# A transformer layer on one core: the feed-forward columns computed only for the tokens that chose them, in sorted order

## What is computed

```python
q = q * cos + rotate_half(q) * sin                 # k likewise
att = softmax(causal((q @ k.T + bias) / sqrt(16)))  # per head
attention = (att @ v) @ Wp + bp

logits  = l2norm(xn) @ l2norm(col_emb).T + sigmoid(gelu(xn @ gate_w1 + gate_b1) @ gate_w2 + gate_b2)
mask    = one_hot(top_1(logits), 16)                # k = max(1, int(16 * 0.05)) = 1
weights = mask * softmax(logits)
cols    = gelu(einsum("bsd,cdn->bscn", xn, W_cols) + b_cols) * weights[..., None]
y       = cols.reshape(-1, 1024) @ proj_w + proj_b + xn
ffn     = layernorm(y) * ln_g + ln_b
```

## Time and profile before

| | |
|---|---|
| median of 3 runs | 2119.47 us (2115.34 to 2126.33) |
| profiled execution | 2120.78 us |
| its span in the profile | 2118.7 us |
| PE busy | 1881.9 us |
| DVE busy | 1602.9 us |
| ACT busy | 1101.7 us |
| POOL busy | 632.2 us |
| first score product | 220 us into the span |
| mean granted PE clock | 0.962 |

### The profile page before, as it was taken

How to read it: one execution, slowest core, us unless ns; L and a number is a source line. 1 busy time by engine, 2 the same in 40 slices (tenths; PEclk the granted TensorE clock), 3 DMA queues, 4 the chain that set the end, 5 groups by cost and what they waited for, 6 DMA issues and landing times.

```text
span 2118.7 us, 41887 instructions
## 1 busy us (share of the span) xinstructions
PE 1881.9 (89%) x11110; PEld 1051.4 (50%) x11110; DVE 1602.9 (76%) x5859; ACT 1101.7 (52%) x2142; POOL 632.2 (30%) x848
## 2 busy tenths in 40 slices
PE   4887899999999999999999999999999999997677
PEld 2654455555445555555455554455555554443223
DVE  2335788888888688878888778887888788887773
ACT  2231555555565555556555455565555555644444
POOL 5463333223333322233333123333332233300000
PEclk9988899999999999999999999999999999998887
DMA  8422212232222122232212222221222322112101
GB/s 221 130 60 76 59 50 65 56 84 81 66 60 72 49 68 64 60 93 68 59 47 69 70 75 66 65 76 47 70 56 64 86 81 60 47 52 58 45 14 41
DMA packets 199400, 144.77 MB, mean 68 GB/s; under 512 B 60427, under 2 KB 186779, under 8 KB 199148
## 3 DMA queue, kind: packets, MB, share of 16 engines
q1 hardware_dynamic: 199148, 141.85, 24.2%
HBM read 90.59 MB, written 56.69 MB: 70 GB/s over the span
## 4 chain that ended last, share of the span: by engine, by line
PE 58%; DVE 21%; issue 11%; POOL 3%; SPq 3%; ACT 3%; DMA 1%; DVEq 0%; ACTq 0%; POOLq 0%
PE scores L1081 10%; PE bank L1092 9%; PE o_bank L1000 8%; PE scores L983 7%; PE bank L1038 5%; DVE scores L1153 5%; PE rows L1020 4%; DVE rows L1178 4%; PE rows L1026 3%; DVE maxima L1174 3%; PE rows L1024 2%; PE scores L1083 2%; PE bank L1110 2%; DVE maxima L1183 2%; ACT probs L869 2%
## 5 line engine op out<-in xcount | busy, mean ns | idle before, releaser
L869 ACT ACTIVATE probs<-scores 128x512 f32<-128x512 f32 (+1 forms) x1280 | 670.7, 555 | 522.5 <-DVE scores L1153 238.4
L983 PE MATMUL scores<-stack_q,stack_k 99*128 99x512 bf16 (+3 forms) x1536 | 439.0, 337 | 85.2 <-ACT probs L869 60.4
L1178 DVE CUSTOM_DVE_ANT_0 rows<-rows,near_rows 128x256 f32<-128x256 f32 (+1 forms) x1024 | 416.1, 409 | 28.3 <-PE rows L1020 24.6
L1153 DVE TENSOR_TENSOR scores<-scores,near_cols 128x256 f32<-128x256 f32 x768 | 333.6, 443 | 84.5 <-PE scores L983 84.0
L1174 DVE TENSOR_REDUCE maxima<-rows 128x1 f32<-128x256 f32 (+1 forms) x768 | 304.9, 397 | 121.4 <-PE rows L1024 119.3
L1000 PE MATMUL o_bank<-probs,v_aug 128*32 128x512 f32 (+3 forms) x3072 | 320.7, 505 | 3.2 <-ACT probs L869 3.2
L1020 PE MATMUL rows<-stack_k,stack_q 96*128 96x256 bf16 (+1 forms) x1024 | 276.2, 276 | 41.5 <-DVE maxima L1178 24.0
L1081 PE MATMUL scores<-xn_t,w_cols 128*128 128x256 f32 x1024 | 286.9, 404 | 2.5 <-ACT others_t L915 2.5
L1183 DVE TENSOR_REDUCE maxima<-rows 128x1 f32<-128x128 f32 (+3 forms) x512 | 248.9, 486 | 50.3 <-PE rows L1026 48.1
L1092 PE MATMUL bank<-w_proj,act_t 128*128 128x256 f32 x1024 | 270.4, 402 | 16.4 <-DVE y L1211 14.7
L983 PEld LDWEIGHTS scores<-stack_q,stack_k 99*128 99x128 bf16 x1536 | 142.3, 99 | 217.4 <-ACT probs L869 138.1
(11 more groups left out here) (109 smaller groups left out, 2270.2 us busy)
## 6 DMA issues: line engine op xcount, KB each, us to landing
parts_d<-part SPq DMA_DIRECT2D x96, 256.0 KB, 2.5
stack_q<-parts_d SPq DMA_DIRECT2D x384, 64.0 KB, 2.6
stack_k<-parts_d SPq DMA_DIRECT2D x384, 64.0 KB, 2.6
x<-in_x_dram SPq DMA_DIRECT2D x32, 256.0 KB, 3.5
v_d<-v SPq DMA_DIRECT2D x32, 256.0 KB, 2.5
rest_d<-rest SPq DMA_DIRECT2D x32, 256.0 KB, 2.7
v_in<-v_d SPq DMA_DIRECT2D x32, 256.0 KB, 3.3
result<-rest_d SPq DMA_DIRECT2D x32, 256.0 KB, 3.9
```

The costliest lines, as they stand in the source:

```text
L869: act.activation(probs[:, (g * NS + s) % PROBS, h, 0:width], ring[(rings + ring_n[1]) % RING][:, 0:width], ACT.Exp, scale=float(D) ** -0.5 ...
L983: ins = pe.matmul(ring[(rings + ring_n[1]) % RING][:, c0:c0 + w], stack_k[g % 2][:, h, kb * P:(kb + 1) * P], stack_q[g % 2][:, h, q0:q0 + ...
L1153: dve.tensor_tensor(tile[:, 0:2 * P], tile[:, 0:2 * P], near, ALU.add))
L1178: dve.tensor_tensor_reduce(tile[:, 0:w], tile[:, 0:w], near_rows[:, ag * GH + h, 2 * P - w:2 * P], 1.0, LOWEST, ALU.add, ALU.max, maxima[: ...
```

## The change

The dense feed-forward part is replaced by a sorted one. When the fourth chunk of a batch has passed the gate (group 2), `tally` and `route` count the tokens of each column (PE products with matrices of ones, DVE arithmetic), give each column whole halves of 64 slots, and each token a slot; 2048 slots a batch, whatever the choice. POOL scatters the 1024 rows of xn to `xs_d` (8 indirect transfers). The following four groups each take 512 slots (`FFN_STEPS`): SP loads them (`ffn_in`), PE turns them (`xs_turn`), `neurons` and `columns` compute each half with its own column's weights, which POOL has gathered one group ahead from a table in DRAM (8 indirect transfers, `weights`), ScalarE scales by the weight, POOL adds xs, SP stores `ys_d`. POOL gathers the rows back by token (`gather`, 2 x 4 transfers); `finish_begun`, `finish_stats` and `finish` do the layer norm just ahead of `project`, and x is read again from DRAM (`again`) in place of `rest_d`. Further: row tiles are packed (`ROW_TILES`, 10 instead of 12 a head, 7 instead of 10 plain reductions), the last two value products, `o_out` and `o_turn` of a group move into the opening of the next (`TAIL`), `shift` moves to slot 34, `shift_turn` to 36, the load of v to its own stage at 28, the store of the parts to slot 37 (`parts`), and POOL's rotation writes into `rot` without the tile `swapped`.

```diff
+SLOT = 64
+WROW = KC * N + C + 1
+SLOTS_B = (T // SLOT + E) * SLOT
+FFN_STEPS = NC
+HALVES = SLOTS_B // SLOT // FFN_STEPS
+PAIRS = HALVES // 2
...
-ROWS = [(qb, part) for qb in range(NT) for part in range(1 if qb < 4 else 2)]
-EARLY = [k for k, (qb, _) in enumerate(ROWS) if qb < NT // 2]
-LATE = [k for k, (qb, _) in enumerate(ROWS) if qb >= NT // 2]
+ROW_TILES = [
+    ([(0, 0, 128, 0), (1, 0, 256, 256)], [("near", 0, 0), ("near", 1, 256)]),
+    ([(2, 128, 384, 0), (3, 256, 512, 256)], [("near", 2, 0), ("near", 3, 256)]),
+    ([(2, 0, 128, 0), (3, 0, 256, 256)], [("far", 2, 0, 128, 1, 1), ("far", 3, 256, 256, 1, 1)]),
+    ([(4, 384, 640, 0), (5, 512, 768, 256)], [("near", 4, 0), ("near", 5, 256)]),
+    ([(6, 640, 896, 0), (7, 768, 1024, 256)], [("near", 6, 0), ("near", 7, 256)]),
+    ([(4, 0, 384, 0)], [("far", 4, 0, 384, 1, 1)]), ([(5, 0, 512, 0)], [("far", 5, 0, 512, 1, 1)]),
+    ([(6, 0, 384, 0)], [("far", 6, 0, 384, 1, 1)]), ([(7, 0, 512, 0)], [("far", 7, 0, 512, 1, 1)]),
+    ([(6, 384, 640, 0), (7, 512, 768, 256)], [("far", 6, 0, 256, 2, 2)])]
+EARLY, LATE = range(3), range(3, len(ROW_TILES))
...
-BESIDE = {1: [('columns', 3)],
-          2: [('widen', None), ('columns', 4)],
-          3: [('center', None)],
-          4: [('columns', 5)],
-          5: [('columns', 6)],
-          6: [('columns', 7)],
-          7: [('x_turn', None)],
-          9: [('y2_stats', None)],
-          10: [('skip', None)],
+ROUTE_STEPS = 14
+WT_LOADS = HALVES
+BESIDE = {2: [('widen', None)],
+          3: [('finish_begun', 0)],
+          6: [('center', None), ('finish_stats', 0)],
+          8: [('x_turn', None)],
+          9: [('finish', 0)],
           11: [('qk_begun', 0), ('qk', 0)],
-          12: [('load_q', None), ('v', 0)],
-          15: [('finish', None), ('qk_begun', 1)],
-          16: [('qk', 1)],
-          17: [('hidden', None)],
-          19: [('v', 1)],
+          12: [('load_q', None)],
+          13: [('v', 0), ('finish_begun', 1)],
+          14: [('xs_turn', 0), ('qk_begun', 1)],
+          15: [('qk', 1)],
+          16: [('xs_turn', 1), ('finish_stats', 1)],
+          18: [('neurons', None), ('hidden', None)],
+          19: [('v', 1), ('finish', 1)],
           21: [('gate', None), ('o_turn', 0)],
+          22: [('columns', 0), ('gather', 1)],
           23: [('qk_turn', 0), ('choose', None)],
+          24: [('columns', 1)],
           25: [('left', 0), ('tie', None), ('middle', 0)],
-          26: [('choice', None), ('y_turn', 0)],
-          28: [('load_k', None), ('project_begun', 0)],
-          29: [('project', 0)],
-          30: [('qk_turn', 1)],
-          31: [('left', 1), ('mask_turn', None)],
-          32: [('y_turn', 1)],
-          34: [('middle', 1)],
-          35: [('project_begun', 1)],
-          37: [('project', 1)]}
-OPENING = [("stats", None), ("columns", 0), ("columns", 1), ("columns", 2)]
-ALONE = ([("stats", None), ("center", None), ("x_turn", None)] + [("columns", k) for k in range(C_PIECES)]
-         + [("qk_begun", 0), ("qk", 0), ("qk_begun", 1), ("qk", 1), ("y2_stats", None), ("skip", None),
-            ("hidden", None), ("v", 0), ("gate", None), ("v", 1), ("choose", None), ("qk_turn", 0),
-            ("left", 0), ("tie", None), ("choice", None), ("finish", None), ("middle", 0), ("qk_turn", 1),
-            ("left", 1), ("mask_turn", None)]
-         + [("neurons", (k, m)) for k in range(2) for m in range(N_PIECES)] + [("middle", 1)]
-         + [("neurons", (k, m)) for k in range(2, 4) for m in range(N_PIECES)])
-CLOSING = [("load", None), ("neurons", (0, 0)), ("neurons", (0, 1)), ("pv", NS - 1), ("o_out", 1),
-           ("neurons", (1, 0)), ("neurons", (1, 1)), ("neurons", (2, 0)), ("shift", None),
-           ("neurons", (2, 1)), ("neurons", (3, 0)), ("neurons", (3, 1)), ("o_turn", 1), ("shift_turn", None)]
+          26: [('choice', None), ('y_turn', 0), ('weights', 0)],
+          27: [('weigh', None), ('gather', 0), ('weights', 1), ('qk_turn', 1)],
+          28: [('load_k', None), ('load_v', None), ('project_begun', 0), ('tally', None), ('weights', 2)],
+          29: [('project', 0), ('left', 1), ('weights', 3)],
+          30: [('weights', 4)],
+          31: [('middle', 1), ('route', None)],
+          32: [('y_turn', 1), ('weights', 5)],
+          33: [('weights', 6), ('weights_routed', 0), ('weights_routed', 1)],
+          34: [('shift', None), ('project_begun', 1), ('weights', 7), ('weights_routed', 2), ('weights_routed', 3)],
+          35: [('weights_routed', 4), ('weights_routed', 5)],
+          36: [('project', 1), ('shift_turn', None), ('weights_routed', 6), ('weights_routed', 7)],
+          37: [('parts', None)]}
+OPENING = [("again", 0), ("ffn_in", None), ("stats", None)]
+ALONE = [("stats", None), ("center", None), ("x_turn", None), ("qk_begun", 0), ("qk", 0), ("qk_begun", 1), ("qk", 1),
+         ("hidden", None), ("v", 0), ("gate", None), ("v", 1), ("choose", None), ("qk_turn", 0), ("left", 0),
+         ("tie", None), ("choice", None), ("weigh", None), ("middle", 0), ("qk_turn", 1), ("left", 1), ("tally", None),
+         ("route", None)] + [("weights", i) for i in range(HALVES)] + [("middle", 1), ("parts", None)]
+FFN_ALONE = ([("ffn_in", None), ("xs_turn", 0), ("xs_turn", 1), ("neurons", None), ("columns", 0), ("columns", 1)]
...
+CLOSING = [("load", None)]
+TAIL = {-2: ("pv", NS - 2), -1: ("pv", NS - 1), 1: ("o_out", 1), 4: ("o_turn", 1)}
...
+                    elif stage == "route":
+                        pool.wait_ge(slots_ready, fb + 1)
+                        alone(pool)
+                        wait(pool, ffn_loaded, fb * (FFN_STEPS * 16))
+                        alone(pool)
+                        if g < 0:
+                            pool.wait_ge(columns_in, LATE_LOADS * 16)
+                        for j in range(NT):
+                            pool.indirect_dma_start(xs_d[:, :], bass.IndirectOffsetOnAxis(slot_i[:, j:j + 1], 0),
+                                                    xn_all[:, j, :], None).then_inc(scattered[j >= CT], 16)
...
+                    elif stage == "weights":
+                        yb, k, step = next_step(b, g)
+                        if arg == 0:
+                            pool.wait_ge(columns_routed, yb + 1)
+                            alone(pool)
+                        pool.indirect_dma_start(wt[:, arg, :], None, wt_d[:, :],
+                                                bass.IndirectOffsetOnAxis(
+                                                    weight_at[:, k * HALVES + arg:k * HALVES + arg + 1], 0)) \
+                            .then_inc(wt_in, 16)
...
+                    elif stage == "gather":
+                        if arg == 0:
+                            wait(pool, gathered, b * (NT * 16))
+                            alone(pool)
+                            pool.tensor_copy(slot_kept[:, :], slot_i[:, :]).then_inc(slots_kept, 1)
+                            pool.wait_ge(slots_kept, b + 1)
+                            alone(pool)
+                            pool.wait_ge(ys_out, (b + 1) * (FFN_STEPS * 16))
+                            alone(pool)
+                        wait(pool, finished, b * NC + 2 * arg)
+                        alone(pool)
+                        for j in range(NT // 2):
+                            at = arg * (NT // 2) + j
+                            pool.indirect_dma_start(gathered_y[:, j, :], None, ys_d[:, :],
+                                                    bass.IndirectOffsetOnAxis(slot_kept[:, at:at + 1], 0)) \
+                                .then_inc(gathered, 16)
...
+                    elif stage == "columns":
+                        yb, k, step = step_of(b, g)
+                        pool.wait_ge(scaled_ys, step * 2 + (arg + 1))
+                        pool.tensor_tensor(ys[:, 2 * arg:2 * arg + 2, :], ys[:, 2 * arg:2 * arg + 2, :],
+                                           xs[:, 2 * arg:2 * arg + 2, 0:C], ALU.add).then_inc(ys_ready, 1)
...
+                    elif stage == "ffn_in":
+                        yb, k, step = step_of(b, g)
+                        if k == 0:
+                            sp.wait_ge(scattered[0], (yb + 1) * (CT * 16))
                             alone(sp)
-                            sp.dma_start(result[:, k], rest_d[b, :, k * CT:(k + 1) * CT, :]) \
-                                .then_inc(rest_in_done[k], 16)
+                            sp.wait_ge(scattered[1], (yb + 1) * ((NT - CT) * 16))
+                            alone(sp)
+                        wait(sp, ys_out, step * 16)
+                        alone(sp)
+                        sp.dma_start(xs[:, :, :], xs_d[k * HALVES * SLOT:(k + 1) * HALVES * SLOT, :]
+                                     .rearrange("(q p) f -> p q f", p=P)).then_inc(ffn_loaded, 16)
...
+                        for qb, k0, k1, at in ROW_TILES[k][0]:
```

(49 more changed lines are left out.)

553 lines of the change are left out of this document (322 added, 231 removed).

## The result

2269.1 us (four runs, 2265.6 to 2273.8) against 2120.3: ratio 1.070, interval 1.067 to 1.074. The kernel is slower by 149 us, where the prediction had it faster by 191. The page of the kernel after, its lines for the engines, PE's clock (`PEclk`, tenths of full speed in 40 equal slices of the span) and the DMA queues (packets, MB, share of the time of the 16 DMA engines).

The account below looks back on a forecast made before the run. PE was taken to set the pace, then DVE at 92%: a batch 208.8 + 6 + 10 = 224.8 us against 245.8. Savings of 142 us in 27 groups and 49 in the prologue, end zero, took 2120.8 to 1930; range 1850 to 2085.

Parts of the forecast that it names:

- the price of an indirect DMA: GpSimd's third-group burst of 20 indirect DMAs, 1.4 us each (bounds 0.2 and 3), delays the next group: 10 us a batch.
- In the other groups 8 gathers ... are free: Outside the third group's burst, the 8 gathers end before the next group's opening and cost nothing.
- At 92%, the middle of the dense rows, that is 208.8.: DVE's 192.1 us a batch, at the 92% busy of the dense score-slot stretches, makes a batch 208.8 us.
- the clock under 0.9: Sign of being wrong: PE's granted clock under 0.9 in the middle slices, pointing to the rival of a falling clock.
- DVE under 85%: Sign of being wrong: DVE under 85% busy without the waits or low clock named, meaning hand-overs not seen.
- prologue -49: Before the main groups: rounds shorten without neurons and columns, less 12 for indirect DMAs and 10 for transfers; 49 us saved.
- the end, "zero": Last five groups without front: about 6 us lost at each of four joints, 12 us more finishing work, net zero.
- The shift gap: Between groups, the carried value products fail to cover the shift chain: 4.5 us more in 27 groups, 2050 us; 13%.
- The clock: PE, less busy, gets a clock of 0.87 and hand-overs stretch 2 us a group: +55, 1985 us; 10%.
- The burst decides: Indirect DMAs in POOL's third-group queue cost 3 us each, making the kernel slower, 2180 us; 11%.
- The work doesn't shrink: Products of 64 columns cost what 256 cost, so PE stays near 54 us a group: 2115 us; 3%.
- Better overlap: DVE reaches 95% and half of the burst is hidden: 211 us a batch, 1850 us; 8%.

Follow-up runs that it names:

- run 6: Kernel after, each of its 240 later weight gathers replaced by two GpSimd multiplications that make no DMA; 2171.9 us (1.024).
- run 2: Kernel after with the 240 weight gathers of the steps after the second left out; 2117.4 us (1.001).
- run 10: Kernel after with no indirect DMA past the first sequence's routing and first two steps' weights, experts' outputs left out; 2093.6 us (0.988).
- run 11: Kernel after without later indirect DMAs, also without weight copies to DRAM, first scatters and weight gathers, and later tally and ranks; 2026.1 us.
- the ballast runs: Each score matmul given twice, in the kernel after and in the kernel after without later indirect DMAs; 2353.3 and 2164.6 us.

## Why the prediction was wrong

**The path down.** From 2269.1: what the weight gathers cost beyond POOL's own time, with their holds of PE's results, 97 us (run 6); POOL's lateness behind them, 55 (runs 2 and 6); scatters and value gathers, 24 (run 10); the prologue's copies and first bursts with the routing arithmetic, 67 (run 11). That leaves 2026 us, still 96 above the 1930 forecast for the whole change. By place, the forecast missed 66 us in the prologue, 243 in the 27 groups from the first shift to the 28th (1743.6 us against 1642.9 before, where 142 less was forecast) and 35 at the end.

**The step that failed first: the price of an indirect DMA.** "I take 10 us a batch" summed what stands behind the burst in POOL's own queue, at 1.4 us each. That mechanism and its size were about right: 1.27 us each, DVE late at the standard deviations, and POOL's lateness 7.0 us a sequence for the weight gathers (248.1 in run 6 against 241.1 in run 2). What the step put at nothing, without a row for it, is a price on another engine: 12.4 us more a sequence (260.5 against 248.1), in which PE's results are held. The bounds of 0.2 and 3 us were bounds on POOL's time, and no row of an engine's own time could bound an effect elsewhere. "In the other groups 8 gathers ... are free" failed for the same reason: the second group fell from 60.1 to 54.3 us when they went, and only to 55.9 with POOL kept as busy.

**The second: "At 92%, the middle of the dense rows, that is 208.8."** The two dense rows were stretches of 36 and 39 us picked for being dense. Over a sequence DVE reached 82%, and taking 268 us from it gave 51. The groups were neither PE's nor DVE's: a us of PE work is worth 0.42 to 0.53, one of DVE 0.19, the rest, by what is left over and not by a run of its own, is hand-overs in order. Without indirect DMAs, but with the routing arithmetic that the sum has too, a sequence takes 236.2 us (run 10), where the sum without its 10 for the burst had 214.8; 21.4 us, six and three quarter times, is 144 us, the largest single error. Of the prediction's signs of being wrong, the clock under 0.9 came true, and so did the last, DVE under 85%, "which would mean hand-overs that I have not seen"; run 10 has it too, with nothing held. The group with least on it, the third row of run 10, did come to the forecast's 54 (54.65).

**The third: prologue -49.** 17 us later instead, 66 off. Without copies and first bursts it would have been 30 earlier (186.0 against 215.5), so the relief, put at 71, was 29.5, and the added transfers and bursts, taken at 22, measured 47. (The 71 has a slip of its own: four rounds of 35 us that become 17 save 72, not 63.)

**The fourth: the end, "zero".** From the 28th shift to the last instruction it is 295.0 us after and 260.3 before, 35 us more. Without the weight gathers it is 263.8 (run 2), with POOL kept as busy 270.9 (run 6), without any indirect DMA 262.5 (run 10): the zero was right but for them.

**The rivals.** *The shift gap* (2050): no; waits for the turned shift total 24.7 us after, under 1 a group. *The clock* (1985): it fell as described, to 0.78 to 0.93 in a sequence, but the ballast runs show no net gain from having it back. *The burst decides* (2180, slower, 11%): the right side and the right place, but with the wrong price; its break-even of 2.6 us of POOL time for each indirect DMA was never reached at 1.27, and the loss came all the same. That the kernel is slower, as this rival had it, is no support for its price. *The work doesn't shrink* (2115): PE did lose 229 us, less than the 11 us a group taken (about 350), part of it since its instructions last longer at the low clock, as the value products of 512 columns at 711 ns instead of 616. PE near 43 us in a group was not seen; it is 47 to 55. *Better overlap* (1850) came nowhere near.

The Trainium skill's figure that I weighed, about 2.0 us fixed for a GpSimd DMA, most of it completion ("DMA: Bandwidth & Descriptors", Anatomy of one DMA), does not hold POOL still: in the trace the next indirect DMA starts 1.27 us after the one before.

One reading in the argument on tile widths was loose: the product 0.35 us behind the value products is the gate's. A row product of full width starts between them, at 1041.17, before their records end at 1041.24. The turn costs even less than was allowed for, and the argument stands.

## What to carry over

Price a kind of instruction that the trace does not hold by what it may do to the other engines, not only to its own queue, and try it alone before a design rests on hundreds of it. Plain DMAs from SyncE's queue moved the same bytes at no cost here, so they are the choice wherever the program can name the rows; if gathers must be on GpSimd, keep their runs short: the holds grow with the run's length, and taking the long runs apart gave 51 of 152 us. And take the worth of relief on one engine from a run with its work thinned (here 0.42 us a us), not from the densest stretch of the next engine.
